# An adapter and expert-FFN kernel whose first tile is loaded by sub-tiles, with batch 0's fold and bias product earlier on TensorE

## The reference

```python
# layer 0: adapter. A = 128, E = 16, D = 512
hidden = gelu(einsum('bsd,ad->bsa', x, down_W) + down_b)
expert_out = einsum('bsa,boa->bso', hidden, expert_W[idx]) + expert_b[idx]
domain_output = where(valid, expert_out, hidden)      # valid: 0 <= id < E
hidden = domain_output + domain_emb[idx]
x1 = layernorm(einsum('bsa,da->bsd', hidden, up_W) + up_b + x) * gamma + beta
# layer 1: feed-forward. E = 8, H = 512, I = 2048
h = gelu(einsum('bsh,bhi->bsi', x1, Wi[e]) + bi[e])
y = layernorm(einsum('bsi,bih->bsh', h, Wo[e]) + bo[e] + x1) * gamma1[e] + beta1[e]
```

## Time and profile before

| | us |
|---|---|
| median of 3 runs | 765.18 |
| lowest, highest | 765.03, 765.25 |
| the profiled execution | 765.08 |
| its span in the trace | 763.3 |
| PE busy | 754.6 |
| POOL busy | 466.8 |
| DVE busy | 509.2 |
| ACT busy | 347.0 |

### The profile page before, as it was taken

How to read it: one execution, slowest core, us unless ns; L and a number is a source line. 1 busy time by engine, 2 the same in 40 slices (tenths; PEclk the granted TensorE clock), 3 DMA queues, 4 the chain that set the end, 5 groups by cost and what they waited for, 6 DMA issues and landing times.

```text
span 763.3 us, 9907 instructions
## 1 busy us (share of the span) xinstructions
PE 754.6 (99%) x3364; PEld 623.9 (82%) x3364; DVE 509.2 (67%) x1049; ACT 347.0 (45%) x610; POOL 466.8 (61%) x398
## 2 busy tenths in 40 slices
PE   8999999999999999999999999999999999999996
PEld 5988888888888888888888888888888888888885
DVE  6618956788468983789836888368874789545116
ACT  4754444444454435534444444453454444343440
POOL 4797564875639564495554965468663775656441
PEclk9999999999999999999999999999999999999999
DMA  8950001200013000155302200022000210001001
GB/s 284 399 198 1 1 0 56 92 19 1 1 69 97 2 0 1 70 169 231 108 31 86 81 1 1 1 97 69 1 1 0 70 43 0 1 15 42 0 1 55
DMA packets 18419, 45.68 MB, mean 60 GB/s; under 512 B 2369, under 2 KB 3777, under 8 KB 17473
## 3 DMA queue, kind: packets, MB, share of 16 engines
q1 hardware_dynamic: 17392, 43.74, 16.3%
q10 hardware_dynamic: 976, 1.31, 0.5%
HBM read 36.66 MB, written 8.39 MB: 59 GB/s over the span
## 4 chain that ended last, share of the span: by engine, by line
PE 97%; SPq 1%; DMA 1%; DVE 0%; ACT 0%; issue 0%; DVEq 0%; ACTq 0%
PE acc L841 15%; PE acc L843 15%; PE acc L842 15%; PE ps_h L841 15%; PE ps_h L843 15%; PE ps_h L842 15%; PE ps L842 2%; PE ps L841 2%; PE ps L843 2%; DMA w_raw<-in_w 0%; DMA ids<-in_ids 0%; PE ps_h L927 0%; SPq L220 0%; ACT wi L486 0%; ACT x1t L477 0%
## 5 line engine op out<-in xcount | busy, mean ns | idle before, releaser
L322 POOL TENSOR_TENSOR wi<-w_raw,wi 128x512 fp32r<-128x512 f32 x128 | 167.7, 1310 | 238.9 <-ACT wi L486 238.5
L507 ACT ACTIVATE h<-ps_h,bi_now 128x512 fp32r<-128x512 f32 x110 | 75.9, 690 | 295.3 <-PE ps_h L843 295.3
L681 DVE TENSOR_TENSOR h<-ps_h,h 128x512 fp32r<-128x512 f32 x124 | 85.4, 689 | 166.0 <-ACT ps_h L508 165.1
L841 PE MATMUL acc<-wo,h 128*128 128x512 f32 x504 | 196.1, 389 | 0.0
L842 PE MATMUL acc<-wo,h 128*128 128x512 f32 x504 | 196.1, 389 | 0.0
L843 PE MATMUL acc<-wo,h 128*128 128x512 f32 x504 | 196.1, 389 | 0.0
L841 PE MATMUL ps_h<-x1t,wi 128*128 128x512 f32 (+1 forms) x504 | 195.2, 387 | 0.0
L842 PE MATMUL ps_h<-x1t,wi 128*128 128x512 f32 (+1 forms) x504 | 195.2, 387 | 0.0
L843 PE MATMUL ps_h<-x1t,wi 128*128 128x512 f32 (+1 forms) x504 | 195.2, 387 | 0.0
L328 POOL TENSOR_TENSOR wo<-w_raw,wo 128x512 fp32r<-128x512 f32 x126 | 162.4, 1289 | 1.4 <-ACT wo L495 1.4
L670 DVE STREAM_TRANSPOSE ps<-rows 32x128 f32<-32x128 f32 x448 | 144.2, 322 | 5.7
(11 more groups left out here) (130 smaller groups left out, 602.7 us busy)
## 6 DMA issues: line engine op xcount, KB each, us to landing
w_raw<-in_w SPq DMA_DIRECT2D x28, 512.0 KB, 9.2
rows<-in_x SPq DMA_DIRECT2D x32, 256.0 KB, 2.7
out<-rows SPq DMA_DIRECT2D x32, 256.0 KB, 2.0
xt_raw<-in_xT SPq DMA_DIRECT2D x7, 1024.0 KB, 4.8
w_raw<-in_w SPq DMA_DIRECT2D x8, 256.0 KB, 4.2
vec<-in_vec SPq DMA_DIRECT2D x2, 768.0 KB, 8.3
xt_raw<-in_xT ACTq DMA_DIRECT2D x2, 256.0 KB, 4.0
vec<-in_vec SPq DMA_DIRECT2D x2, 256.0 KB, 5.5
```

Source lines behind the costliest of these rows:

```text
L322: pool.tensor_tensor(slot[:, 1], w_raw[:, c, 0, :].rearrange("p (k i) -> p k i", k=KD), slot[:, 0].bitcast(F32), ALU.subtract).then_inc(wi ...
L507: act.activation(h_slot(t, c)[:, 0, :], bank, ACT.Gelu, bias=bias)
L681: dve.tensor_tensor(h_slot(t, c)[:, 1, :], hidden_bank(t, c), h_slot(t, c)[:, 0, :].bitcast(F32), ALU.subtract).then_inc(h_split, 1)
L841: pe.matmul(out, left[0], right[0], start=start, stop=False)
```

## The change

xT of tile 0 comes from an array of its own, `xT0`, laid out by sub-tiles: part s is sub-tile s with all four feature chunks, one run of 2 KB per partition. `first_down(s)` is then four matmuls of 128 columns that need one part, where it was two matmuls of 256 columns for each of two parts. Part 2 and part 3 are issued by SP with the load of `beta` between them.

The indices come as one row on one partition in place of 128 copies. `valid` is made on one partition (`flags`), spread to all 128 by a matmul of ones with `flags` (PE), and copied out of PSUM by DVE behind the split of the down weights. `WARM` goes from (7, 1, 1) to (5, 2): five matmuls before the spreading one, two behind it, and none later.

Expert 0's block comes in one load of 259 columns, where it was 131 columns early and 128 columns late.

On PE, sub-tile 0's expert product comes in the middle of sub-tile 1's down product, sub-tile 0's up product before sub-tile 1's expert product, and `fold_product(0)` and `bias_product(0)` behind sub-tile 1's up product, into the banks of `acc` for sub-tiles 3 and 2. So `first_up(2)` waits for `bias_copied` and `first_up(3)` for `fold_copied`, while the waits on them before `early_products(1, 1)` and `turn(3)` are gone. ACT and POOL are reordered to match.

```diff
-WARM = (7, 1, 1)
+WARM = (5, 2)
...
-            return ps0[:, 0, :] if b else ps_h[:, 1, :]
+            return ps0[:, 0, :] if b else acc[:, 3, :]
...
+        def first_part(s):
+            return xt_raw.rearrange("p k t -> p (k t)")[:, s * D:(s + 1) * D]
+        def first_bank(s):
+            return ps0[:, s % 2, s * P:(s + 1) * P]
...
-            sp.dma_start(exp_raw[:, 0, 0:A + 3], exp_d[e0[0], :, 0:A + 3]).then_inc(exp_landed[0], 16)
+            sp.dma_start(exp_raw[:, 0, :], exp_d[e0[0], :, :]).then_inc(exp_landed[0], 16)
...
             first_xt(2)
+            sp.dma_start(vec0[:, 1, :], vec0_d[:, 2, :]).then_inc(beta_landed, 16)
             first_xt(3)
-            sp.dma_start(vec0[:, 1, :], vec0_d[:, 2, :]).then_inc(beta_landed, 16)
-            sp.dma_start(exp_raw[:, 0, A + 3:], exp_d[e0[0], :, A + 3:]).then_inc(fold_exp_landed, 16)
...
             pool.wait_ge(up_b_landed, 16)
+            expert_weights(0)
             add_raw_bias(1)
             inverse_root(0, 0, 0)
             add_raw_bias(2)
-            expert_weights(0)
...
+            dve.wait_ge(flags_spread, 1)
+            dve.tensor_copy(valid[:, :, :], acc[:, 3, 0:2 * BATCH].rearrange("p (i b) -> p i b", b=BATCH)).then_inc(valid_ready, 1)
...
-                act.wait_ge(down_done, s // 2 * 2 + 2)
-                act.activation(first_gelu(s), ps0[:, s // 2, s * P:(s + 1) * P], ACT.Gelu,
+                act.wait_ge(down_done, s + 1)
+                act.activation(first_gelu(s), first_bank(s), ACT.Gelu,
...
-                for k in (j % 2 * 2, j % 2 * 2 + 1):
-                    last = pe.matmul(ps0[:, j // 2, half(j)], down_raw[:, k * A:(k + 1) * A], xt_raw[:, k, half(j)],
+                wait(pe, hid_first, s - 1)
+                for k in ks:
+                    down = pe.matmul(first_bank(s), down_raw[:, k * A:(k + 1) * A], first_part(s)[:, k * P:(k + 1) * P],
...
             keep_warm(WARM[0], ps_h[:, 1, :])
+            pe.wait_ge(flags_ready, 1)
+            pe.matmul(acc[:, 3, 0:2 * BATCH], ones, flags[:, :], start=True, stop=True).then_inc(flags_spread, 1)
+            keep_warm(WARM[1], ps_h[:, 1, :])
...
-        "ids": np.concatenate([np.asarray(itok_B_0_15), np.asarray(itok_B_0_7)]).reshape(1, 2 * BATCH).repeat(P, axis=0),
+        "ids": np.concatenate([np.asarray(itok_B_0_15), np.asarray(itok_B_0_7)]).reshape(1, 2 * BATCH),
```

More of the change, by code:

```diff
@@ L90, in adapter_ffn @@
         fold_copy = [rows[:, 1, 1 + b, :] for b in range(BATCH)]
+        flags = sb("flags", [P, 2 * BATCH])
         valid = sb("valid", [P, 2, BATCH])
-        ids = sb("ids", [P, 4, BATCH], I32)
-        idx = sb("idx", [P, 2, BATCH], I32)
+        ids = sb("ids", [1, 4, BATCH], I32)
+        idx = sb("idx", [1, 2, BATCH], I32)
         warm = sb("warm", [P, 1])
@@ L120, in first_expert @@
             return w_raw[:, CH - 2, 0, s * P:(s + 1) * P]
-        def half(j):
-            return slice(j // 2 * HALF, (j // 2 + 1) * HALF)
-        def pair(j):
-            return slice(j % 2 * 2, j % 2 * 2 + 2)
+        def first_part(s):
+            return xt_raw.rearrange("p k t -> p (k t)")[:, s * D:(s + 1) * D]
+        def first_bank(s):
+            return ps0[:, s % 2, s * P:(s + 1) * P]
         def h_slot(t, c):
@@ L433, in _ @@
             for j in (0, 1):
-                act.dma_start(xt_raw[:, pair(j), half(j)], xT_d[0, :, pair(j), half(j)]).then_inc(xt_first[j], 16)
+                act.dma_start(first_part(j), xT0_d[j, :, :]).then_inc(xt_first[j], 16)
             act.dma_start(up_raw, upW_d).then_inc(up_landed, 16)
@@ L532, in _ @@
             first_hidden(0)
+            first_mid(0)
             first_hidden(1)
-            first_mid(0)
             first_mid(1)
+            expert_scale(0, exp_landed[0])
             expert_bias(0)
-            expert_scale(0, fold_exp_landed)
+            fold_round(0)
+            copy_bias(0, acc[:, 2, :])
             first_hidden(2)
@@ L541, in _ @@
             first_mid(3)
+            x1t_round(0, 0, 0)
             wi_round(0, 0, 0)
@@ L598, in _ @@
             dve.memset(ones, 1.0).then_inc(ones_ready, 1)
+            step(dve.memset(flags[:, :], 0.0))
             dve.wait_ge(ids_landed, 16)
@@ L604, in _ @@
             dve.tensor_scalar(idx[:, 1, :], ids[:, 3, :], 0.0, float(E1 - 1), ALU.max, ALU.min).then_inc(idx_ready, 1)
-            is_valid, is_not = valid[:, 0, :], valid[:, 1, :]
+            is_valid, is_not = flags[0:1, 0:BATCH], flags[0:1, BATCH:2 * BATCH]
             step(dve.tensor_scalar(is_valid, ids[:, 0, :], 0.0, None, ALU.is_ge))
@@ L882, in adapter_down, with first_down @@
                       k == 0, k == KD - 1).then_inc(down_done, 1)
-            def first_down(j):
-                if j == 0:
+            def first_down(s, ks=range(KD)):
+                if s == 0:
                     pe.wait_ge(down_landed, 16)
-                pe.wait_ge(xt_first[j], 16)
-                for k in (j % 2 * 2, j % 2 * 2 + 1):
-                    last = pe.matmul(ps0[:, j // 2, half(j)], down_raw[:, k * A:(k + 1) * A], xt_raw[:, k, half(j)],
+                pe.wait_ge(xt_first[s], 16)
+                wait(pe, hid_first, s - 1)
+                for k in ks:
+                    down = pe.matmul(first_bank(s), down_raw[:, k * A:(k + 1) * A], first_part(s)[:, k * P:(k + 1) * P],
                                      start=k == 0, stop=k == KD - 1)
-                last.then_inc(down_done, 1)
+                if k == KD - 1:
+                    down.then_inc(down_done, 1)
             def first_mid(s):
```

32 lines of the change are left out of this document (14 added, 18 removed).

## The result

| | before | after |
|---|---|---|
| median, lowest, highest of 11 runs, us | 765.12, 764.85, 765.62 | 767.13, 766.26, 770.27 |
| ratio of the medians, 95% interval | | 1.0034, 1.0026 to 1.0043 |
| the profiled execution, us | 765.08 | 768.41 |
| its span, us | 763.3 | 766.6 |

The change makes the kernel 2.0 us slower. Its executions fall into two groups: seven with a mean granted clock of 0.997 to 1.000 took 766.26 to 767.23 us (median 766.9), four with 0.993 to 0.995 took 768.41 to 770.27. The profiled execution is one of the four, so its times carry a clock loss that most executions don't have.

What follows compares the result with a forecast made beforehand. PE was taken as the bound, with POOL's chain within 0.3 us; POOL's delay of 2.35 us less 0.31 idle starts the steady loop 2.0 later: 765.08 + 2.0 = 767.1 us, range 766.0 to 768.2.

Steps and rivals of the forecast that it cites:

- the mechanism that it leaned on: Opening: fold and bias product on PE, 12.5 to 14.05, delay sub-tiles 2 and 3's down products, ACT's rounding and POOL.
- The bound: Before `turn(3)`: PE and POOL arrive together, two chains within 0.3 us of each other, both to be followed.
- The size: POOL's first weight-chunk rest 2.35 us later, at 18.6; less 0.31 idle time, the steady loop starts 2.0 us later.
- The 0.48 that it gave to `x1t_round(0)`: ACT: this copy now precedes the first weight rounding, from 17.35, and takes 0.48 us.
- 1.02 - 0.59 for a pair: PE: source given for 0.43 us per up-product instruction, so up product 0 ends at 10.61.
- The head: Opening up to expert 0's block: index gain and larger block taken together as zero, plus or minus 0.4 us.
- The index load: Opening: one row in place of 128 gains 0 to 0.4 us; with the skill's 2.0 us, 0.43 and a sum of 766.6.
- The larger block: Opening: expert 0's block, doubled to about 130 KB, costs 0 to 0.4 us.
- My 5.7 for the first down product: PE: it starts at about 5.7 instead of 4.90, behind the flags, is done by 7.7, and nothing is lost.
- rival (b): PE's opening: TensorE's clock rises later; 767.9 if at about 10.6, 769.2 if behind the bias product; chance 0.12.
- (a): Opening: the head moves 0.4 us earlier, 766.7; with 0.3 us more from overlapping steps, 766.3; chance 0.2.
- (c): Not slower: POOL starts its first rest by 15.9, only the missing bias product counts, 764.4; chance 0.08.

Runs made afterwards that it cites:

- the first experiment: The changed kernel with nine more warm matmuls on PE between sub-tile 1's half down product and sub-tile 0's expert product: 767.30 us, ratio 1.0031.
- the bridge: Nine warm matmuls added on PE before sub-tile 0's expert product; the changed kernel with them took 767.30 us, and 765.83 with fold, bias product and ACT's order put back.
- the move alone: The kernel before with only fold and bias product behind `first_up(1)`, ACT's and POOL's changed orders and the block in one load: 766.28 us, ratio 1.0019.

## Why the prediction was right, and where its steps were not

The number was right: 767.1 forecast, 767.13 measured, slower than before by more than 0.2%. So was the mechanism that it leaned on. Its parts in turn, with the terms that were wrong:

**The bound.** Two chains within 0.3 us of each other, PE and POOL, and the change lets POOL's decide. Shown: PE waits 0.49 us for DVE before `turn(3)`, POOL is without a gap for 7.7 us (20.03 to 27.72), and taking ACT's rounding forward gave back 1.06 us.

**The size.** Forecast: POOL's first rest 2.35 us later, 0.31 of it taken up by idle time, the steady loop 2.0 later. Against sub-tile 0's expert product, with an undisturbed clock, the rest came 2.42 us later (9.99 - 7.57) and the steady loop 1.94. The sum was good to 0.1 us. It didn't say how much of it belongs to the move and how much to the rest of the change; the runs give 1.63 and 0.31 by the traces. The order of sub-tiles 0 and 1 alone is worth 0.71 us by medians in a kernel without the move and with a later block, so 0.31 is not its price everywhere. The 0.48 that it gave to `x1t_round(0)` ahead of the first rounding came to 0.61, of which 0.50 is the step itself (18.14 to 18.64). One term has a wrong source: the 0.59 in "1.02 - 0.59 for a pair" stands in no row of PE, but the 0.43 per instruction that comes of it is right (in the first experiment's trace the up product at 17.95 lets the next matmul start at 18.81, 0.86 for the pair). By medians the move is worth 1.75 between undisturbed runs, 1.47 with the bridge, and 1.1 alone in the kernel before.

**The head.** The sum was right (8.65 against 8.68) by luck: both of its terms were much too small. The index load was given 0 to 0.4 us and brought 1.2. The step that failed: from 2 KB in 2.4 us and 256 KB in 2.7 I concluded that nothing but a fixed time was left. Both rows are loads over 128 partitions, and neither shows a load of one row. (With 2.0 us in place of the row's 2.4 the sum is 766.7, not 766.6.) The larger block was given 0 to 0.4 us and took 1.1 more. There even the cause was wrong: half the bytes took 4.3 us, the whole block 3.1 once the two loads of ACT were behind it. Two errors of about 1 us cancelled: the block landed at about 7.8 in the profiles of both kernels and of the move alone, issued at 3.16, 4.34 and 4.51 (at 7.2 to 8.0 in the others with its neighbours ahead of it), and at 6.2 once they were out of its way. My 5.7 for the first down product was 4.76 because the indices came earlier; what came of that is under the clock.

**The clock, rival (b).** It was given 0.12 and happened in 4 of 11 executions, in another form: I had it rise late, as at the start; in the profiled execution it fell again behind an idle time of PE that was 2.10 us long. For the other three only the lower mean clock is known. I had put the idle time at 0.5 us, since I let the first down products start late and run slowly. The profiled execution paid for it from sub-tile 1 on: sub-tile 1's expert product at 11.76 where 10.61 was forecast, the steady loop at 37.03 where 35.7 was. Without these executions the median would be 766.9. So that the forecast hit the median to 0.03 us is luck: its price was 0.2 us too high, and the clock loss of four executions, which it left out, lifts the median by that much.

**Rivals (a) and (c)** didn't happen. (c) needed POOL's first rest by 15.9; without a clock loss it comes 9.99 us behind 8.65, at 18.6 (an estimate from two traces), which is the forecast's own number.

**Left open.** What makes the block's time to landing differ from run to run by some tenths (4.0 to 4.8 us in five kernels with the same head), and why PE's slow start lasts as long as it does in a given execution. It may decide whether the clock falls later: where the twelve down products took 2.75 us instead of 1.79, less idle time is left behind them. Whether the moved products or ACT's order of `x1t_round(0)` costs more in the median was not tried either. That the slow start made the first experiment no faster is read from one trace, not shown by a run of its own.

## What to carry to other kernels

An instruction that is moved into a gap of one engine also delays what is issued behind it there, and the price is paid by the engine at the end of that chain: follow it through every queue to the first work of the engine that has no idle time left, here POOL. If such a move is wanted, put the later engine's feeding steps (here ACT's rounding of the weight chunks, the second as well as the first) ahead of what now arrives late. And before a load is made earlier, look for the next transfer that would bind: 1.2 us at the index ended as nothing at the first product, and 1.3 us at the first product as 0.3 at the steady loop.

## What the runs showed of the hardware

- A load of 16 bytes on one partition was in DVE's hands 1.3 us after its issue began (0.7 to 2.03), the same indices on 128 partitions 2.4 to 2.6 us after theirs. The Trainium skill, "DMA: Bandwidth & Descriptors", section on the anatomy of one DMA, has a fixed cost of about 2.0 us for a transfer issued by GpSimd; for this one, issued by SP, the measured 1.3 decides.
- The expert block took 3.0 to 3.1 us with two loads of 256 KB behind it on its own queue (three kernels), 4.0 to 4.8 with these issued ahead of it on another (five kernels, 129.5 KB; 4.3 for 65.5 KB), and 4.7 to 5.5 with them issued on another 0.5 and 0.1 us ahead of it (three kernels). Issued 1.2 to 1.35 us later than in the five, it took 3.5 (65.5 KB) and 3.3 (129.5 KB). The same page of the Trainium skill, section on latency, has the latency of memory grow under load; the runs agree in direction.
- Behind 2.10 and 2.25 us without a matmul the granted clock was 0.56 and 0.60 from 8.60 to 9.90, where PE began again, and 0.50 after that, until about 12; behind 2.75 us it was 1.00 for 1.7 us of work and then 0.50 for 7. These are three profiled executions. Most runs of the same kernels have a mean clock of 0.997 to 1.000 and no such loss; a lower mean (0.996) also occurs once in a kernel whose profile has 0.82 us of idle time there and once in the kernel before. The fall cost 1.5 to 3.9 us, from the median of the undisturbed runs of a kernel to its runs with a lower clock. At the program's start PE is slow as well (weight loads of 333 ns instead of 192), for a time that differs from run to run, and the granted clock does not show it.
